# A clearing operation on GpSimd ahead of each of 384 indirect DMAs: other kind, other places

## The reference, cut to what matters

```python
x = x + xattn(layernorm(x), ctx, ctx, mask)     # 16 heads of 16, 77 context rows
h = layernorm(x)
scores = sigmoid(h @ gate_weight.T); sfc = scores + bias          # 32 experts in 8 groups
# the 4 best groups by their best expert, then the 6 best experts in them
tw = scores of the chosen / their sum * 2.5
routed = sum over the 6 chosen experts e of tw[e] * (silu(h @ gate_e.T) * (h @ up_e.T)) @ down_e.T
x = x + routed + shared_expert(h)
```

## Time and profile before

| what | us |
|---|---|
| median of 3 runs (869.93 to 871.14) | 870.69 |
| the profiled execution, its own time | 878.87 |
| its span | 877.2 |
| POOL busy in the span | 517.3 (59%) |
| PE busy in the span | 768.9 (88%) |
| DVE busy / ACT busy in the span | 500.7 / 393.0 |

### The profile page before, as it was taken

The page is one execution under the profiler, slowest core; times in us unless marked ns, Lnnn a source line. Parts: engine busy times, 40 slices in busy tenths (PEclk is TensorE's granted clock), DMA queues, the critical chain, the costliest instruction groups (busy, mean ns, idle before and its releaser), DMA issues.

```text
span 877.2 us, 17678 instructions
## 1 busy us (share of the span) xinstructions
PE 768.9 (88%) x5472; PEld 658.4 (75%) x5472; DVE 500.7 (57%) x1556; ACT 393.0 (45%) x822; POOL 517.3 (59%) x603
## 2 busy tenths in 40 slices
PE   4699989988899999959997999999999999899920
PEld 2488877777777777624655999999999998799920
DVE  4667666666666667522345223367666665466652
ACT  1264444444444444210111566666666665466610
POOL 0204777777777777777000000778888887888885
PEclk9698888899988888678999899999999999899965
DMA  9113444444444322245513355888888898788852
GB/s 292 42 46 112 132 133 139 138 137 138 139 141 153 120 84 90 103 152 196 188 49 96 110 172 165 239 249 267 262 269 264 258 268 250 209 247 261 257 156 72
DMA packets 120222, 149.01 MB, mean 170 GB/s; under 512 B 17265, under 2 KB 106741, under 8 KB 120002
## 3 DMA queue, kind: packets, MB, share of 16 engines
q1 hardware_dynamic: 99416, 94.33, 34.4%
q0 software_dynamic: 19200, 52.45, 19.9%
q10 hardware_dynamic: 1514, 1.09, 0.5%
HBM read 80.56 MB, written 67.26 MB: 169 GB/s over the span
## 4 chain that ended last, share of the span: by engine, by line
PE 39%; POOL 31%; issue 17%; SPq 4%; DVE 4%; DMA 4%; ACTq 1%; ACT 0%; POOLq 0%; DVEq 0%
POOL rows L480 19%; PE sc_ps L892 16%; PE bank L902 8%; PE sc_ps L787 6%; POOL hold L469 5%; PE sc_ps L876 4%; POOL work L513 3%; PE bank L798 3%; POOL rstd L487 2%; DMA work<-yrows,dest 2%; SPq L429 2%; SPq L423 1%; DVE stats L924 1%; DMA yrows<-work 1%; DMA wdn<-in_gate_b 1%
## 5 line engine op out<-in xcount | busy, mean ns | idle before, releaser
L513 POOL DMA_INDIRECT work<-yrows,dest x192 | 196.8, 1025 | 59.5 <-issue 26.8
L892 PE MATMUL sc_ps<-work 128*128 128x128 f32 x1792 | 222.4, 278 | 3.6 <-DVE work L1332 3.6
L480 POOL DMA_INDIRECT rows<-work,dest x192 | 189.4, 986 | 57.5 <-issue 47.7
L892 PEld LDWEIGHTS sc_ps<-work 128*128 128x128 f32 x1792 | 212.9, 195 | 4.0 <-issue 3.8
L469 POOL TENSOR_TENSOR hold<-cst 128x1 f32<-128x1 f32 x160 | 98.3, 615 | 138.7 <-DMA yrows<-work 134.5
L902 PE MATMUL bank<-wdn,work 128*128 x448 | 117.1, 384 | 7.6 <-DVE work L1287 7.6
L1313 DVE SCALAR_TENSOR_TENSOR work<-work 128x256 f32<-128x256 f32 x160 | 77.3, 483 | 57.2 <-DMA work<-yrows,dest 49.9
L1287 DVE TENSOR_TENSOR work<-work,sc_ps 128x256 f32<-128x256 f32 x112 | 46.9, 419 | 103.0 <-ACT work L613 80.0
L635 ACT ACTIVATE work<-bank 128x512 f32<-128x512 f32 x112 | 66.8, 596 | 52.7 <-PE bank L902 34.5
L902 PEld LDWEIGHTS bank<-wdn,work 128*128 128x128 f32 x448 | 77.1, 192 | 15.2 <-issue 9.3
L613 ACT ACTIVATE work<-sc_ps 128x256 f32<-128x256 f32 x112 | 42.9, 383 | 77.7 <-PE sc_ps L892 70.2
(11 more groups left out here) (163 smaller groups left out, 1098.1 us busy)
## 6 DMA issues: line engine op xcount, KB each, us to landing
work<-rows SPq DMA_DIRECT2D x224, 128.0 KB
yrows<-work SPq DMA_DIRECT2D x224, 128.0 KB
wgu<-in_egu SPq DMA_DIRECT2D x16, 512.0 KB
store<-in_x SPq DMA_DIRECT2D x8, 512.0 KB, 10.1
x1d<-work SPq DMA_DIRECT2D x32, 128.0 KB
wdn<-in_edn SPq DMA_DIRECT2D x8, 512.0 KB
work<-x1d SPq DMA_DIRECT2D x8, 512.0 KB, 3.7
out<-work SPq DMA_DIRECT2D x32, 128.0 KB
```

Of the source, the lines that this page charges most:

```text
L480: pool.indirect_dma_start(rows[:, :], bass.IndirectOffsetOnAxis(ap=dest[:, t, k:k + 1], axis=0), rowb[:, m, :], None).then_inc(scat[m], 16)
L513: pool.indirect_dma_start(yg[:, g % RG, :], None, yrows[0:n * P, :], bass.IndirectOffsetOnAxis(ap=dest[:, t, k:k + 1], axis=0)).then_inc(l ...
L892: last = mm(ps8[2 + m % 2][:, (2 * w + g) * P:(2 * w + g + 1) * P], wst[w][m % 2][:, k * 2 * I + g * I:k * 2 * I + (g + 1) * I], xeT[:, m ...
```

## The change: what it does

`pause()` becomes a memset of 128 x 128 fp32 zeros to `hold`, which grows from one column to 128. The wait for its semaphore moves: each memset waits for the memset before it (the first waits for nothing), and no DMA waits for its own memset any more. A pause stands ahead of each of the 192 scatters and each of the 192 gathers, 384 in all.

```diff
-        hold = sb("hold", [P, 1])
+        hold = sb("hold", [P, P])
...
-            pauses = itertools.count(1)
+            pauses = itertools.count()
 
             def pause():
-                pool.tensor_tensor(hold[:, :], const("ones")[:, 0:1], const("half_neg")[:, 0:1],
-                                   ALU.pow).then_inc(S_["pause"], 1)
-                pool.wait_ge(S_["pause"], next(pauses))
+                done = next(pauses)
+                if done:
+                    pool.wait_ge(S_["pause"], done)
+                pool.memset(hold[:, :], 0.0).then_inc(S_["pause"], 1)
...
-                    pause()
                     for k in range(half * TOPK // 2, (half + 1) * TOPK // 2):
+                        pause()
                         pool.indirect_dma_start(rows[:, :], bass.IndirectOffsetOnAxis(ap=dest[:, t, k:k + 1], axis=0),
                                                 rowb[:, m, :], None).then_inc(scat[m], 16)
...
-                    if g % 2 == 0:
-                        pause()
+                    pause()
                     pool.indirect_dma_start(yg[:, g % RG, :], None, yrows[0:n * P, :],
                                             bass.IndirectOffsetOnAxis(ap=dest[:, t, k:k + 1], axis=0)
                                             ).then_inc(ld_y[g % RG], 16)
```

## The result

The changed kernel is slower. Its median is 923.28 us in 4 runs (920.98 to 929.31), against 870.31 us in 4 runs of the kernel before: ratio 1.0626, with a 95% interval of 1.0569 to 1.0683. 844 us was forecast. The time is also far over rival 4, the slower one (891 us).

What follows compares the result with a forecast made beforehand. POOL was taken to bound the gathers and 14 attention steps; -1.4 us from scatters and -25.6 us from gathers, limited by PE, made -27.0 us, scaled to -26.7 us: 844 us, range 835 to 866 us.

Steps and rivals of the forecast that it cites:

- rival 4: Clearing ahead of each DMA not short: 0.40 us each, gathers and scatter steps longer, 891 us; chance 0.14.
- c: POOL time added per DMA by its memset: 0.18 us plus 0.02 us behind a DMA, 0.20 us.
- 1.26: Gap and duration of a DMA on POOL, 0.30 + 0.96 us, kept unchanged for a DMA behind a memset.
- the sum: Whole kernel: scatters -1.4 us in 14 attention steps, gathers -25.6 us, in all -27.0 us in the profiled execution.
- rival 3: Memset vanishes in the gap ahead of each DMA; scatter steps gain 8.7 us, about -34 us, 837 us; chance 0.08.
- Rival 1: Memsets held up 0.09 us each beside DVE's work in the gathers: -15.8 us, 855 us; chance 0.13.
- But then PE is late next: Gather stage: PE at 3.09 us per pair ends its last block at 832.3, so the last gather starts at 843.1.
- Rival 5: Gathers can't go faster, DMA engines being 80 to 90% busy; only scatters move, 869 us; chance 0.07.
- the slack of those steps: Attention stage: 18 of 32 `rstd` waited for DVE, with slack up to 2 us, so POOL's gains don't count there.

Runs made afterwards that it cites:

- e5: Changed kernel with a memset of 448 one-byte elements in place of 128 fp32: 877.47 us, 1.0073 of the kernel before.
- e6: Changed kernel with a memset of 384 one-byte elements in place of 128 fp32: 861.39 us, 0.9897 of the kernel before.
- e7: Changed kernel with a memset of 320 one-byte elements in place of 128 fp32: 851.43 us, 0.9784 of the kernel before.
- r1: The changed kernel, unedited, on a chip where the kernel before takes 854.14 us: 827.74 us, 0.9715 of it.
- r2: The kernel before, unedited, on the same chip as r1: 853.88 us, ratio 0.9997.
- s2: Changed kernel with 320 one-byte elements, as e7, on a chip where the kernel before takes 852.97 us: 841.43 us, 0.9857.
- e1: Changed kernel, but each DMA waits for the memset ahead of it: 889.16 us, 1.0171 of the kernel before.
- e4: Kernel before with its old clearings in the old 160 places, only the wait moved as in the change: 868.25 us, 0.9914 of the kernel before.
- e9: Changed kernel with 320 one-byte elements ahead of scatters and 352 ahead of gathers: 848.87 us, 0.9927 of the kernel before.
- s1: Changed kernel without any clearing, on a chip where the kernel before takes 868.9 us: 943.09 us, 1.0876 of it.
- e2: Changed kernel with a memset of 512 one-byte elements in place of 128 fp32, still without a wait: 897.61 us, 1.0268 of the kernel before.

## Why the prediction was wrong

**What bounds the kernel: right.** POOL was saturated in the gathers, and where its distance shrank with nothing else in the way (e5 to e6, and the right column until PE's pace) the time fell at about the forecast rate.

**The cost of the clearing, c = 0.20 us: too high.** The memset takes 0.22 us (0.219 median in the gathers), longer than the 0.18 taken, but 0.14 us of it vanish in the gap of 0.30 us, which the prediction took to belong to the DMA itself: behind a memset the DMA starts after 0.16. A gather comes every 1.34 us where 1.26 + c was meant to be 1.46 (or the 1.498 that the sum had, counted on from the old mean), so c is 0.08. That is part of rival 3. Rival 1 fell: by the median the memset takes 0.219 us in the gathers and 0.220 in the scatters (means 0.228 and 0.219), nowhere near 0.09 us longer beside DVE's work. With the Trainium skill, "SBUF — State Buffer", section "Who interferes with whom", an engine that only writes isn't held by DVE's second input; the two numbers agree. The same section says that PE and ACT never wait on anyone for those memory ports. The trace agrees in that PE's matmuls at 699.85, 700.72 and 701.15 start without a gap; the rule is not about the notice that they are done.

**The step that failed** is "But then PE is late next. Its last block pair leaves ScalarE at 842.4 now; from 489.3 with 111 steps of 3.09 us it would be 832.3". It took PE's pace with gathers 1.67 us apart for its pace with gathers at any distance. At 1.34 us it came out at 3.69 us per pair, the last block at 897.0 for 832.3, and the last gather at 910.8 for 843.1. The cheaper clearing, which the sum counted as pure gain, made it this bad. But the step fails at the 1.50 us that the sum had as well. e7 has that distance and measured 851.43 us where 870.33 is before, -18.9 for the forecast -26.7 us, and that they are so near is luck. PE took 3.16 us per pair, and the gathers 313.6 us from first to last, 6.8 less than before, where the sum had 25.6 less. The other 20.8 us came ahead of the first gather, where the sum had 1.4. All five rivals were about what one clearing costs or what POOL waits for; none asked what POOL's DMAs do to others when they come closer. Rival 5, full DMA engines, is answered by r1: the same share of 0.89 as before, and gathers of 0.965 us. Rival 4, on the slower side, had its cause in c and decided from 0.32 us on; c came out at 0.08, and the kernel was slower still.

**Where PE keeps its pace** the forecast stands: r1 against r2 is 825.50 to 852.48 us in the profiled executions, -27.0 us, for the -27.0 of the sum, and 0.9715 is 2.9% where 3.1% was forecast. The parts are not those of the sum, though. The gathers give 19.9 us (295.7 for 315.6 us from first to last) instead of 25.6. The stages ahead of them give 7.0 (first gather at 519.6 for 526.6) instead of 1.4, since a clearing of 0.08 us also shortens the scatters, as rival 3 had it (8.7 us). That the total agrees to the tenth is luck; that it has this size is not.

**Scatters.** The steps of the first measurement hardly changed: from first to last `rstd` the mean is 10.10 us for 10.28. The shorter clearing moved the wait to the variance, from 18 waits to 25. The prediction had put the slack of those steps at up to 2 us; without the longest, the waits of the earlier trace rows average 2.6 us, and late notices were in them. e6 and e7, with 1.5 us and more ahead of *every* scatter, do better than before, though POOL's own work per step is no shorter: their last scatter is at 398.4 and 389.2 us for 403.3. e7 waits for the variance 9 times instead of 18. So evenly spaced DMAs were faster than three in a row and a pause. Late notices are the likely reason: there are 59 before and none in e5, e6 and e7. From the kernel before to 320 elements the mean step falls from 10.28 to 9.73 us on the chips of the left column, and on those of the right, where no notice is late, it stays (9.64 in r2, 9.71 in s2).

**What stays open.** What holds PE's notices while POOL issues indirect DMAs, and what differs between chips, no run tells. The counts of late notices are lower bounds, since records are missing on the chips with the longer times: in the gather stage 224 of 273 are there in the kernel after, 126 in e6, 133 in e5. The count of ACT's L613 has no such holes and falls in the same order of distances. How late a notice is doesn't say what it costs: e1 has nearly as many late ones as the kernel after and loses 1.7%, e4 has 66 and gains. Late notices cost little as long as the queues behind them don't run dry, which is an argument and wasn't tested. Whether fewer rows per DMA move the limit wasn't tried.

## What to carry to other kernels

Before making an engine's DMA issue denser, ask what the present spacing protects: write the start-to-start distance next to the pace, and try a version at the old distance and one between. A wait that "another engine ends late" deserves the question why that engine is late, above all if it ends together with other waits just behind the last DMA of a string. And measure such a change on more than one chip: here its sign depends on it. The version to take is a clearing of 320 one-byte elements ahead of each DMA: 0.978 of the time before on a chip where close DMAs cost time, 0.986 where they don't. By the stages on the first kind, 320 ahead of scatters and 352 or 384 ahead of gathers might be a little better; e9, made for that, ran on the other kind. The change itself gives 0.972 on the latter, but 1.063 on the former.

## What the runs showed of the hardware

- On the chips of the left column PE's completions reached ACT and DVE late, by up to 5.0 us in the kernel after and 6.2 us in s1 (ACT's L613), while POOL issued indirect DMAs of 128 rows one closely behind the other. In the gathers 95 to 107 records were late at 1.25 to 1.44 us, 43 at 1.50, 6 at 1.55 and none at 1.60 and 1.66; in the scatters none from 1.52 us on, but for 2 in e2. Of the 107 of the kernel after 83 came while POOL made no DMA, in the median 0.96 us behind its last. It cost 6.3% at 1.34 us and 8.8% at 1.25 us. A quarter of the bytes changes nothing (1.067).
- On the chips of the right column none was late at any distance from 1.25 us on (nine profiles; ACT's L613, where ACT was idle, started 0.04 us behind the modelled end).
- A memset on POOL costs by elements, not bytes: 0.219 us for 128 fp32, 0.357 for 288 one-byte elements, 0.384 for 320, 0.437 for 384, 0.490 for 448, 0.544 for 512, that is 0.83 ns per element and 0.12 us beside.
- Behind a memset that nobody waits for, an indirect DMA starts after 0.16 us; behind a waited one after 0.27; behind another DMA after 0.30.
- Chips differ by 2% with the kernel before (868.9 to 875.9, and 853.0 to 855.4 us). The granted clock isn't it: the kernel before has 1.00 from 620 to 713 us on both sides.
